# Identity products in 17 waits of the tensor engine around an attention's first and last periods, and four steps moved

## The reference

```
x = x + 0.5 * ffn(layernorm(x));  x = x + attn(layernorm(x));  x = x + 0.5 * ffn(layernorm(x))

attn: 16 heads of 16, 64 landmarks (means over 8 tokens) q_l, k_l
  s1 = softmax(q @ k_l^T);  s2 = softmax(q_l @ k_l^T);  s3 = softmax(q_l @ k^T)
  z = s2^T / (max col sum * max row sum);  6 times: xz = s2 @ z
      z = 0.25 * z @ (13 I - xz @ (15 I - xz @ (7 I - xz)))
  out = (s1 @ (z @ (s3 @ v))) @ Wo + bo
ffn: a shared SwiGLU (512 wide) + one of 8 experts per token (argmax of x @ gate_w^T), weighted by a sigmoid
```

## Time and profile before

| | |
|---|---|
| median of 3 runs | 1158.67 us (1156.79 to 1158.83) |
| the profiled execution | 1158.67 us, of which the span from first to last instruction is 1156.6 us |
| PE busy | 1088.4 us, 94% of the span |
| DVE, ACT, POOL busy | 764.1, 582.8, 553.8 us |
| mean granted clock of PE | 0.977 of full |

### The profile page before, as it was taken

How to read it: one execution, slowest core, us unless ns; L and a number is a source line. 1 busy time by engine, 2 the same in 40 slices (tenths; PEclk the granted TensorE clock), 3 DMA queues, 4 the chain that set the end, 5 groups by cost and what they waited for, 6 DMA issues and landing times.

```text
span 1156.6 us, 30028 instructions
## 1 busy us (share of the span) xinstructions
PE 1088.4 (94%) x11278; PEld 882.3 (76%) x11279; DVE 764.1 (66%) x1411; ACT 582.8 (50%) x961; POOL 553.8 (48%) x764
## 2 busy tenths in 40 slices
PE   7999999999999678999999999779999999999997
PEld 5788887888888556677777777558888887888886
DVE  5736746666766557768878877655346566667674
ACT  4344336656665344555555464334443256566663
POOL 5720734666665623444543541316301725666664
PEclk9999999999999878999999999889999999999999
DMA  7272144222221210000000000104241242212220
GB/s 254 73 301 100 37 143 144 64 73 68 63 65 38 92 56 2 3 3 3 4 3 3 3 3 3 39 3 182 92 182 37 74 159 69 63 62 61 73 64 15
DMA packets 39471, 80.24 MB, mean 69 GB/s; under 512 B 6452, under 2 KB 31159, under 8 KB 38336
## 3 DMA queue, kind: packets, MB, share of 16 engines
q1 hardware_dynamic: 27568, 52.94, 12.7%
q0 software_dynamic: 11232, 25.20, 7.0%
q10 hardware_dynamic: 560, 0.52, 0.1%
HBM read 57.13 MB, written 27.00 MB: 73 GB/s over the span
## 4 chain that ended last, share of the span: by engine, by line
PE 80%; DVE 10%; ACT 4%; issue 3%; DMA 1%; POOL 1%; DVEq 0%; ACTq 0%; POOLq 0%; SPq 0%
PE PS L1840 18%; PE PS L1754 13%; PE PS L1854 11%; PE PS L1770 7%; PE PS L1928 3%; PE PS L1847 3%; PE PS L1685 2%; PE PS L2051 2%; PE PS L1788 2%; ACT XNT L1258 2%; PE PS L2072 2%; DVE A_NM L799 2%; PE PS L2038 2%; PE PS L1781 1%; PE PS L1989 1%
## 5 line engine op out<-in xcount | busy, mean ns | idle before, releaser
L1840 PE MATMUL PS<-WHL,XGH 128*128 128x512 f32 x624 | 217.4, 430 | 0.6 <-DVE WHL L680 0.6
L1854 PE MATMUL PS<-WD,XNT 128*128 x624 | 149.6, 383 | 2.5 <-ACT XNT L1177 1.5
L1584 POOL TENSOR_TENSOR A_W<-A_XC,CB 128x256 f32<-128x256 f32 x86 | 61.8, 737 | 170.1 <-DVE A_XC L897 155.4
L701 DVE SCALAR_TENSOR_TENSOR XNT<-PS,SCORES,XNT 128x512 f32<-128x512 f32 x78 | 58.6, 751 | 119.6 <-PE PS L1840 103.4
L1491 POOL DMA_INDIRECT X<-xs_dram,WHO x78 | 99.4, 1274 | 57.6 <-issue 23.1
L1172 ACT ACTIVATE XNT<-PS,SCORES 128x512 f32<-128x512 f32 x78 | 53.7, 688 | 143.6 <-PE PS L1840 126.7
L1840 PEld LDWEIGHTS PS<-WHL,XGH 128*128 128x128 f32 x624 | 111.4, 189 | 18.9 <-DVE WHL L680 1.1
L1854 PEld LDWEIGHTS PS<-WD,XNT 128*128 128x128 f32 x624 | 112.6, 190 | 17.1 <-issue 3.4
L1840 PE MATMUL PS<-WHL,XGL 128*128 128x512 f32 x312 | 123.2, 395 | 0.0
L1485 POOL TENSOR_SCALAR XNT<-WD 128x128 f32<-128x128 f32 x64 | 52.5, 839 | 128.9 <-DVE WD L574 128.9
L1770 PE MATMUL PS<-SDH,HHL 128*128 128x256 f32 x512 | 104.0, 287 | 1.7 <-DVE X L614 1.3
(11 more groups left out here) (273 smaller groups left out, 2537.9 us busy)
## 6 DMA issues: line engine op xcount, KB each, us to landing
xs_dram<-WG SPq DMA_DIRECT2D x16, 512.0 KB, 3.0
WU<-in_r_up SPq DMA_DIRECT2D x2, 4096.0 KB, 13.8
shared_dram<-X SPq DMA_DIRECT2D x16, 512.0 KB, 2.9
WG<-in_r_gate SPq DMA_DIRECT2D x2, 4096.0 KB, 16.4
WD<-in_r_down SPq DMA_DIRECT2D x4, 2048.0 KB
X<-in_x SPq DMA_DIRECT2D x7, 512.0 KB, 9.1
X<-mid_dram SPq DMA_DIRECT2D x7, 512.0 KB, 3.9
X<-xs_dram,WHO POOLq DMA_INDIRECT x78
```

Of the source, the lines that this page charges most:

```text
L701: dve.scalar_tensor_tensor(B["RH"][:, u * F:(u + 1) * F], banks[3 + u][:], score(t), B["RS"][:, u * F:(u + 1) * F], ALU.mult, ALU.mult).th ...
L1584: pool.tensor_tensor(B["W"][:].rearrange("p (a m) -> p a m", m=M)[:, part, :], B["XC"][b % 2][:].rearrange("p (a w) -> p a w", w=XW)[:, pa ...
L1840: ins = pe.matmul(banks[bank][:], tok, w[:, k * F:(k + 1) * F], start=(k == 0 and i == 0), stop=(k == KD - 1 and i == 2))
L1854: ins = pe.matmul(banks[7][:, 0:D], B["HT"][:, u * F + f * P:u * F + (f + 1) * P], B["WD"][:, bass.ds(ex * (KF * D) + f * D, D)], start=(f ...
```

## The change

It adds a function `fill(bank, n)` on PE, n products of the identity with itself into a bank that is free there, and calls it in front of or behind waits: in seven places ahead of period 0 (5, 4, 4, 2, 2, 5 and 4 products), in periods 0 and 1 (4 each), in period 6 (4, 4 and 5) and in period 7 (3, 6, 3, 6 and 4). It moves steps: in period 7 the statistics of batch 5 on DVE from ahead of the fifth step's `chain_s` to behind its `chain_x`, and the high parts of batch 6 on ACT ahead of the last `chain_b`; in periods 0 and 1 the rounding of the keys ahead of the turned tokens; in every period with a next batch the copy of the sums on ACT ahead of the last `chain_b`, and their turn on PE ahead of the first `s1_max` and so of the last `chain_second`; in period 0 PE's first turn of batch 2 ahead of the first `chain_second`.

```diff
--- before.py
+++ after.py
@@ -1023,7 +1023,7 @@
                 masked_scale(b)
                 if exists(nxt):
                     row_sums(nxt)
-                if exists(done):
+                if exists(done) and b < NG - 1:
                     wait_alone(att["xo"], count("xo", done, 2))
                     stats(done, 1)
                 chain_s(b, 4)
@@ -1038,6 +1038,9 @@
                 if exists(nxt):
                     column_max(nxt)
                 chain_x(b, 4)
+                if b == NG - 1:
+                    wait_alone(att["xo"], count("xo", done, 2))
+                    stats(done, 1)
                 if exists(nxt):
                     pair_scale(nxt)
                 if exists(old):
@@ -1363,9 +1366,11 @@
                     numerators(old, 1)
                 if exists(nxt):
                     key_landmarks(nxt)
+                    if b < 2:
+                        rounded(nxt, 3)
                 if exists(far):
                     turned(far, 0)
-                if exists(nxt):
+                if exists(nxt) and b >= 2:
                     rounded(nxt, 3)
                 chain_b(b, 1)
                 if exists(far):
@@ -1396,10 +1401,12 @@
                     rounded(far, 0)
                     projected(far, 2)
                     rounded(far, 1)
+                if exists(nxt):
+                    sums_kept(nxt, 1)
+                if b == NG - 1:
+                    high_outputs(old)
                 chain_b(b, 5)
-                if exists(nxt):
-                    sums_kept(nxt, 1)
-                if exists(old):
+                if exists(old) and b < NG - 1:
                     high_outputs(old)
                 if exists(nxt):
                     product_kept(nxt)
@@ -2081,6 +2088,10 @@
                                         start=True, stop=True)
                 ins.then_inc(att["recb_ready"], 1)
 
+            def fill(bank, n):
+                for _ in range(n):
+                    pe.matmul(banks[bank][:, 0:P], ident, ident, start=True, stop=True)
+
             pe.wait_ge(s_x[0], 32)
             for _ in range(REWARM):
                 pe.matmul(banks[1][:, 0:2 * P], ident, CB[:, 0:2 * P], start=True, stop=True)
@@ -2089,6 +2100,7 @@
                 nxt, far = b + 1, b + 2
 
                 if exists(nxt):
+                    fill(1, 5)
                     pe.wait_ge(att["bdr"], count("bdr", nxt, 1))
                     pe.wait_ge(att["qkr"], count("qkr", nxt, 3))
                     s3_max(nxt, 0)
@@ -2105,10 +2117,12 @@
                     turn(far, 0)
                     turn(far, 1)
                 if exists(nxt):
+                    fill(1, 4)
                     pe.wait_ge(att["s3m"], count("s3m", nxt, 4))
                     pe.wait_ge(att["kls"], count("kls", nxt, 1))
                     s2_scores(nxt)
                     turn_nm3(nxt)
+                    fill(1, 4)
                     pe.wait_ge(s_picks, 5)
                     pe.wait_ge(att["nm3"], count("nm3", nxt, 1))
                     pe.wait_ge(att["s2s"], count("s2s", nxt, 1))
@@ -2122,6 +2136,7 @@
                     if far == 0:
                         pe.wait_ge(s_low, 4)
                 if exists(nxt):
+                    fill(1, 2)
                     pe.wait_ge(att["qk"], count("qk", far, 1))
                     pe.wait_ge(att["e3"], count("e3", nxt, 2))
                     pe.wait_ge(s_zero, 4)
@@ -2164,6 +2181,7 @@
                     start_t(nxt)
                     pe.wait_ge(att["qk"], count("qk", far, 4))
                     turn_nm1(nxt)
+                    fill(6, 4)
 
             for b in range(NG):
                 done, old, nxt, far = b - 2, b - 1, b + 1, b + 2
@@ -2191,8 +2209,12 @@
                     heads(old, 0)
                     pe.wait_ge(att["nm1"], count("nm1", b, 1))
                     heads(old, 1)
+                if b == 0:
+                    pe.wait_ge(att["xn"], count("xn", far, GT))
+                    pe.wait_ge(att["tm"], count("tm", b, 1))
+                    turn(far, 0)
                 chain_second(b, 0)
-                if exists(far):
+                if exists(far) and b > 0:
                     pe.wait_ge(att["xn"], count("xn", far, GT))
                     pe.wait_ge(att["num"], count("num", old, 1))
                     pe.wait_ge(att["tm"], count("tm", b, 1))
@@ -2208,6 +2230,9 @@
                     s3_max(nxt, 1)
 
                 chain_first(b, 1)
+                if b == NG - 1:
+                    pe.wait_ge(att["num"], count("num", old, 1))
+                    fill(6, 3)
                 if exists(far):
                     pe.wait_ge(att["xo"], count("xo", done, 1))
                     pe.wait_ge(att["num"], count("num", old, 2))
@@ -2219,6 +2244,8 @@
                     pe.wait_ge(att["num"], count("num", old, 1))
                     project_v(nxt, 0)
                 chain_second(b, 1)
+                if b == NG - 1:
+                    fill(6, 6)
                 if exists(nxt):
                     pe.wait_ge(att["s3m"], count("s3m", nxt, 4))
                     pe.wait_ge(att["kls"], count("kls", nxt, 1))
@@ -2236,11 +2263,16 @@
                     turn_nm3(nxt)
 
                 chain_first(b, 2)
+                if b == NG - 1:
+                    fill(6, 3)
                 if exists(nxt):
                     pe.wait_ge(att["nm3"], count("nm3", nxt, 1))
                     pe.wait_ge(att["s2s"], count("s2s", nxt, 1))
                     s3_turned(nxt, 0)
                 chain_second(b, 2)
+                if not exists(done):
+                    pe.wait_ge(att["v_sb"], count("v_sb", nxt, 2))
+                    fill(7, 4)
                 if exists(done):
                     pe.wait_ge(att["v_sb"], count("v_sb", nxt, 2))
                     pe.wait_ge(att["xo"], count("xo", done, 1))
@@ -2255,9 +2287,14 @@
                 pe.wait_ge(att["e3"], count("e3", nxt, 2))
                 s1_turned(b, 0)
                 chain_second(b, 3)
+                if b == NG - 1:
+                    fill(6, 6)
                 if exists(far):
                     pe.wait_ge(att["tts"], count("tts", nxt, 1))
                     project_qk(far, 1)
+                if b == NG - 2:
+                    pe.wait_ge(att["tts"], count("tts", nxt, 1))
+                    fill(6, 4)
                 if exists(nxt):
                     pe.wait_ge(att["e1"], count("e1", b, 2))
                     s3_turned(nxt, 1)
@@ -2291,6 +2330,9 @@
                 if exists(far):
                     pe.wait_ge(att["cs"], count("cs", nxt, 1))
                     project_qk(far, 2)
+                if b == NG - 2:
+                    pe.wait_ge(att["cs"], count("cs", nxt, 1))
+                    fill(6, 4)
                 if exists(nxt):
                     pe.wait_ge(att["ot"], count("ot", old, 2))
                     pe.wait_ge(att["e1"], count("e1", b, 4))
@@ -2298,6 +2340,10 @@
 
                 chain_first(b, 5)
                 if exists(nxt):
+                    pe.wait_ge(att["qk"], count("qk", far, 3))
+                    pe.wait_ge(att["tts"], count("tts", nxt, 2))
+                    pe.wait_ge(att["cs"], count("cs", nxt, 1))
+                    turn_sums(nxt)
                     pe.wait_ge(att["y0"], count("y0", nxt, 2))
                     pe.wait_ge(att["bdr"], count("bdr", nxt, 2))
                     s1_max(nxt, 0)
@@ -2305,11 +2351,8 @@
                     pe.wait_ge(att["ot"], count("ot", old, 2))
                     first_turn(1)
                 chain_second(b, 5)
-                if exists(nxt):
-                    pe.wait_ge(att["qk"], count("qk", far, 3))
-                    pe.wait_ge(att["tts"], count("tts", nxt, 2))
-                    pe.wait_ge(att["cs"], count("cs", nxt, 1))
-                    turn_sums(nxt)
+                if b == NG - 2:
+                    fill(7, 5)
                 if exists(far):
                     pe.wait_ge(att["tts"], count("tts", nxt, 2))
                     project_qk(far, 3)
```

More of the change, by code:

```diff
@@ L1398, in attention_scalar @@
                     rounded(far, 1)
-                chain_b(b, 5)
                 if exists(nxt):
                     sums_kept(nxt, 1)
-                if exists(old):
+                if b == NG - 1:
+                    high_outputs(old)
+                chain_b(b, 5)
+                if exists(old) and b < NG - 1:
                     high_outputs(old)
```

## The result

The changed kernel takes 1146.43 us (median of 4 runs, 1145.14 to 1149.53), the kernel before 1158.75 us beside it: a ratio of 0.9899, with a 95% interval of 0.9872 to 0.9926. The forecast was 1148.3. The profiled execution took 1146.8 us, its span 1144.7, against 1156.6 before.

What follows compares the result with a forecast made beforehand. It took PE to bound the kernel, with time lost where it waits or runs at low clock in the attention. Gains of 2.8 + 0.8 + 1.6 + 5.2 = 10.4 us off 1158.67 gave 1148.3, with 1143 to 1154.

Steps and rivals of the forecast that it cites:

- rival (3): Weight load and stream don't overlap, so an identity product costs 0.45 us and the places overshoot by 8.7; 1156.6 us, chance 0.05.
- (a): Ahead of period 0, the 24 products for batch 0's values run at full clock: 1.6 us gained (1.2 to 1.6).
- (b): Scores and first projection after 412 us, ahead of period 0, run at a higher clock: 0.9 us gained (0 to 2.2).
- (c): The pair of products ahead of the row maxima, where PE has no wait: 0.4 us lost (0 to 0.9).
- Periods 0 and 1: Keys' rounding moved ahead gives 0.4 us; clock still falls in period 0, 0.4 of up to 2.2 taken; sum 0.8.
- plus or minus 3.2, value 0: PE's 1.6 us issue stop in period 5, low clock after it: moved instructions may remove it or make another.
- (e): Period 7: the third first product and its second run at full instead of low clock, 1.1 us gained.
- (f): Period 7: the 2.78 us output projection becomes shorter at full clock than DVE's 1.8 us step, 0.9 us gained.
- (g): Period 7: statistics and high parts moved, batch 6's projection starts 3.2 us earlier (2.0 to 3.6), 1.5 from the statistics.
- (h): End of the attention: the heads of batch 7 run partly at low clock before; no gain taken (0 to 1.6 us).
- (1): Rival: the clock is held everywhere, period 0 too; 1143 us or less, chance 0.06.
- (2): Rival: the clock falls as before, identity products being too little, and only the orders gain; 1155.7 us, chance 0.10.

Runs made afterwards that it cites:

- before_again: The kernel before, unaltered, executed a second time; batch 0's first sums stand 29.6 us behind the restart, where the first profile had 30.3.
- combined: The change with the edits of `stats_back` and `period0_filled` and without the pair ahead of the row maxima; 1138.50 us, ratio 0.9863 to before.
- period0_filled: The change plus 4 products ahead of period 0's turn and 8 ahead of its second first product; 1139.87 us, ratio 0.9880 to before.
- high_back: The change with the high parts of batch 6 put back behind the last BU on ACT; ratio 0.9915 to before.
- products_only: All 69 identity products added to the kernel before, none of the moved steps; 1145.69 us, ratio 0.9935.
- stats_back: The change with the statistics of batch 5 put back ahead of the chain's fifth step; 1139.87 us, ratio 0.9870 to before.
- moves_only: The moved steps of the change without any identity product; 1149.32 us, ratio 0.9962 to before.
- before_shifted: The kernel before with 34 tiny products (8 rows by 8 columns) right behind the restart; 1166.66 us in a single execution.

## Why the prediction was right, and where it was not

**The price of a product: right.** Ten records of five products take 1.27 us after the change, of which 0.27 is the last one's drain, so 0.11 each, as in the slot table. The rule of the rival (3), load plus stream, is not what happens; no place but the pair overshot, as forecast, and the doubled products show what overshoot costs. (Added up again from the listed waits, the overshoot that (3) would give is 9.4 us and not 8.7; nothing hangs on it.)

```profile
402.77 1.27 PE L2093 MATMUL PS<-CB 128*128 128x128 f32 x10
404.54 0.51 PE L1952 MATMUL PS<-A_KTR,A_QBDR 32*128 32x512 f32 x4 [0.49 <-ACT A_QBDR L1307]
```

A wait of 1.6 us has become 1.3 of products and 0.5 of waiting, and the 24 products behind it run at full clock.

**(a) and (b): mechanism right, 1.0 short.** I halved (b) for the transposes between the products; the clock held through, 1.00 from 404.5 to 443.5, and gave 3.5 us against 2.5. But the profiled execution of before was also the longest of three at this place: it took 30.3 to the first sums, `before_again` 29.6 and the moves alone 28.1, so of the 3.5 between 1.3 and 3.5 are the change's. **(c)** 0.4 lost, as priced: the pair has no wait behind it, and without it (`combined`) this part is 0.45 us shorter.

**Periods 0 and 1: the place named, the size short.** The clock fell where I said, for want of products. It fell for 3.5 us and not for 10, and the two periods gave 1.6 instead of 0.8. What a held clock is worth there I put at up to 2.2; less the 0.4 that I counted, 1.8 were left, and `period0_filled` gave 1.85. That the two agree is in part luck, since mine was reckoned for 10 us at the low clock and the run removed 3.5.

**Every period: right at 0.** Periods 3 and 4 last 42.26 and 42.63 us after and 42.27 and 42.65 before; the two groups of maxima start 3.2 us apart in every kernel, as DVE has it.

**Period 5 and 6: the unknown counted.** The term "plus or minus 3.2, value 0" came out at +3.2 in period 5, with new stops worth about 0.8 each in periods 2 and 6; 1.6 in all. The one in period 6 stands in the denominators, which were to gain 1.6. They took 3.13 us after and 3.28 before, so the stop ate what the clock gave back there; in `high_back`, without the stop, they took 1.96. The period as a whole gained 1.0.

**(e) and (f): right**, 2.0 against 2.0.

**(g): the sum and its links right (2.9 for 3.2), its split wrong.** Counted from the fifth first product, the heads were to start at 7.34 us and started at 7.36, and the projection was to start at 11.25 and started at 11.55. The step that failed is "of which 1.5 is the statistics and the rest the order on ACT": I never worked out either order with the other one left as it was. Four kernels whose PE work from the fifth first product to the projection runs at full clock give the split (us; no other moved step lies in this stretch):

| | high parts behind BU | high parts ahead of BU |
|---|---|---|
| statistics ahead of the step | 12.88 (`products_only`) | 10.45 (`stats_back`) |
| statistics behind XC | 12.59 (`high_back`) | 11.55 (the change) |

By themselves the order on ACT gives 2.4 and the statistics 0.3; both together give 1.3, since with the high parts moved the statistics delay the heads that release them. The other 1.6 of the 2.9 is the clock, for which I had no term here. In the first profile of before the spread took 1.23 us and the denominators 3.02; in the second, which is at full clock here, they took 0.73 and 1.96, and fifth first product to projection is 12.85 instead of 14.45:

```profile
761.73 0.78 PE L2038 MATMUL PS<-A_XC,A_W 64*64 64x80 f32 x32 [1.84 <-DVE A_W L903]
...
767.84 1.96 PE L2072 MATMUL PS<-XNT,A_DSEL 128*32 128x128 f32 x64
...
774.58 0.36 PE L1685 MATMUL PS<-A_WOH,A_OTH 128*128 128x256 f32 x1 [2.44 <-POOL A_OTL L1606]
```

**(h)** I took nothing for the heads; they ran at full clock, 1.5 of at most 1.6. This is the moves' doing and not the products'. Where PE waits 2.2 to 2.5 us for the low parts (both profiles of before, `products_only`, `high_back`), the clock falls in the wait or within 1.5 us of its end, and the part takes 5.7 to 6.7 us; where the wait is 0.9 us or none, `moves_only` included, it takes 4.2. `before_shifted` alone has the long wait and 4.2.

**The sum.** 10.4 forecast; 15.2 in the stretch of two profiled executions, 11.9 in their span, 12.3 by the medians. That the total came so near is in part luck: the stretch gave 4.8 more than the terms, 3.2 of it from the stop in period 5, which I had counted at 0 either way, and the FFNs, which the change leaves alone, took 3.3 more in this execution. The rival nearest in the number is (1): the clock is held everywhere but in period 0, and `period0_filled`, which holds it there too, gains another 1.9 us by the stretch and 2.9 by the times. The test of (2) is `moves_only`: the orders alone gave 4.4 us, where I priced them 4.0 (less 1.0 for the pair and the overshoot, which that kernel doesn't have).

## What to carry to other kernels

Where an engine's clock falls between short groups of work, fill its waits with products that it would have had time for, count them by the record (here 0.11 us) against each wait as it will be afterwards, and leave none where there is no wait: 69 gave 7.5 us, and twice as many gave 7.7 back. When two steps are moved at once, work out each order with the other already moved; the sum can be right while one of the two costs. And compare profiles by parts and more than one execution: here a stop that no edit aimed at was worth 3 us, as much as a whole part of the change, and the place of a low clock in one execution up to 2.

## What the hardware showed that was not expected

- Transposes of the identity hold the granted clock in these waits as well as fp32 products do (stretch 377.1 against 376.8 to 377.0).
- PE stops for 0.3 to 1.6 us without a wait at places that go with the position in its instruction stream: the 26th of 64 records in period 5 of three profiles, 1.29 to 1.57 us; gone there with 34 tiny products put in 300 us earlier. All 28 such stops end 2.2 to 2.8 us after a 16 KB transfer of the instruction queue began. A stop of 1.3 or 1.6 us was followed by 3.4 us of low clock in both profiles of before, and by none in `moves_only`.
- A product of 8 rows by 8 columns isn't cheap: 34 of them took 11.6 us behind the restart, 0.17 us a record, for most of it at the low clock. A record of an identity product, 128 by 128, takes 0.11 at the full one.
